# A four-layer graph network: adjacency and its transpose in one load, masks on GpSimd, and another order of work

## The chip, the cores and the metric

The kernel runs on one NeuronCore of a Trainium2 chip. The core has five engines with their own instruction streams: TensorE (PE in the profile; its weight loads are PEld), VectorE (DVE), ScalarE (ACT), GpSimd (POOL) and SyncE (SP), which here issues every transfer. They run their streams in order and wait for one another on semaphores. The metric is the time of one execution on the device, in microseconds; lower is better. Of several runs the median counts.

## The reference

128 graphs of 128 nodes with 512 features go through four graph attention layers. Each layer normalises its input, clips it at zero, makes a score for each pair of nodes, masks the scores by the adjacency, and adds the attention-weighted features to its input:

```python
h = jnp.maximum(_layernorm(x, axis=-1), 0.0)
x = x + _L0_gnn_ref(h, adj, W, a1, a2)          # 1 head, mask adj
h = jnp.maximum(_layernorm(x, axis=-1), 0.0)
x = x + _L1_gnn_ref(adj, h, W1, ..., W2, ...)   # 4 heads of 256, elu, then 1 head
h = jnp.maximum(_layernorm(x, axis=-1), 0.0)
x = x + _L2_gnn_ref(h, adj, w_src, w_dst, b)    # 1 head, mask adj + identity
h = jnp.maximum(_layernorm(x, axis=-1), 0.0)
x = x + _L3_gnn_ref(h, adj, W_proj, W_att, b)   # 8 heads of 64
```

Layer 1 has two attention layers (L1a with W1, L1b with W2), takes the softmax over the source nodes with `mask = (adj > 0) | eye`, and so needs the mask turned. Layer 3 takes its softmax over the second node, with the mask as it is; the kernel works on its scores turned as well.

## The kernel before

One graph fills the 128 partitions. The kernel is a software pipeline over graphs: each engine has a loop over `step`, and in it a fixed list of calls, each for the graph that stands so many steps behind. The whole schedule is that list, one for each engine, and the semaphores; nothing decides at run time.

```python
for step in range(G + SKEW):          # G = 128, SKEW = 12
    t = Turn(G, step)
    project_L1b_first_high(t, t.graph(5))   # graph number step - 5
```

I write `name(5)` for a call on the graph 5 steps behind. In a step `L0` works on graph 2 behind, `L1a` on 3 and 4, `L1b` on 5, `L2` on 6 and 7, `L3` on 9 to 11; the result of graph 12 behind is stored. PE stops being fully fed at the two ends of the loop, when the first graphs have not reached the late layers or the last ones have left the early layers.

Masks. GpSimd's `make_mask` (L1475) turns the int32 adjacency into 0 or -5e9 in bf16. `make_mask_loop` (L1482) clears the diagonal. PE turns both by a product with an identity: `turn_mask` (L450) and `turn_mask_L3` (L735), both into `bank_a`, which the products of L0 and L2 use too; ScalarE copies them to SBUF in `copy_mask` (L844) and `copy_mask_L3` (L990). The turned mask with cleared diagonal goes into `masked_L1a` and `masked_L1b`, the turned one into `masked_L3`.

Scores. For each attention the row of target scores of a graph goes from VectorE (`rows_...`, a 32x32 transpose) to DRAM (`send_...`) and comes back spread over all partitions (`spread_...`, L296 and L344): 64 KB for one head, 256 KB for L1a, 512 KB for L3. L3 needs a second round: VectorE takes eight masked maxima (`most_L3`, L1329), and their row goes out and back as `send_shift_L3`, `spread_shift_L3` (1 MB, L344). GpSimd adds the mask (`masked_...`), ScalarE does leaky relu and exp (`leaky_...`, `exp_...`), GpSimd subtracts the shift in L3 (`shift_L3`, L1540).

PE turns the exponentials (`turn_exp_L2` L493, `turn_prob_L1a` L579) and multiplies (`product_...`; L3's is L741, L1a's is L585). The wide projections (L432) split each float32 operand in a high and a low part: `hT_hi` on ScalarE, `hT_lo` on VectorE, three products for each weight. `scale_and_bias` (L1449, L1451, L1454) makes the layer norm's factors on GpSimd from VectorE's `stats` and `moments`.

At the end of L3, `result_L3` (L1372) on VectorE frees `bank_e`, for which `project_L3_last_high(9)` waits by its semaphore `out_read`; `out_L3` (L1558) adds the residual on GpSimd.

Of the kernel before, what the change touches and what calls it, by code (L numbers as in the profile page):

```python
# [14 lines left out]
SKEW = 12  # L15
# [39 lines left out]
def build(nc, x, adj, a0_w, a0_a1, a0_a2, w1, b1, w2, b2, attn_src, attn_dst, attn_b, w_proj, b_att, ident_in,  # L55
# [20 lines left out]
    with ExitStack() as ctx:  # L76
# [15 lines left out]
        identb = sb("identb", [P, P], BF16)  # L92
# [17 lines left out]
        PR, VR = 2, 2  # L110
        x_in = sb("x_in", [P, XR, D])
        adj_in = sb("adj_in", [P, XR, P], I32)
        mask = sb("mask", [P, MR, P], BF16)
        mask_loop = sb("mask_loop", [P, LR, P], BF16)
        mask_turned = sb("mask_turned", [P, TR, P], BF16)
        mask_flat_turned = sb("mask_flat_turned", [P, PR, P], BF16)
# [107 lines left out]
        def _(sp):  # L224
# [17 lines left out]
            def load_graph(s, i):  # L242
                sp.dma_start(x_in[:, s, :], x[i]).then_inc(sem(f"x_loaded{s}"), 16)
                sp.dma_start(adj_in[:, s, :], adj[i]).then_inc(sem(f"x_loaded{s}"), 16)
# [53 lines left out]
            def send_L0(g):  # L298
                send_one("L0", g, 0)
# [55 lines left out]
            for step in range(G + SKEW):  # L355
                t = Turn(G, step)
                load(t.graph(0))
                store(t.graph(12))
                spread_L2(t.graph(7))
                send_L0(t.later_graph(2))  # L360
                spread_L0(t.later_graph(2))
                send_L1b(t.graph(5))
                send_shift_L3(t.graph(10))
                spread_L1b(t.graph(5))
                spread_shift_L3(t.graph(10))
                send_L1a(t.graph(3))
                spread_L1a(t.graph(3))
                send_L3(t.graph(9))
                send_L2(t.graph(6))
                spread_L3(t.graph(9))  # L370
# [4 lines left out]
        def _(pe):  # L375
# [44 lines left out]
            pe.wait_ge(sem("setup_pe"), 2)  # L420
# [17 lines left out]
            def turn_mask(t, g):  # L438
                if g.live:
                    pe.wait_ge(sem("masks_made"), g.made())  # L440
                    if t.full:
                        pe.wait_ge(sem("x1_made"), g.made())
                    else:
                        pe.wait_ge(sem("mask_copied"), g.made(1))
                        pe.wait_ge(sem("L0_pT"), g.made())
                        pe.wait_ge(sem("x1_made"), g.made())
                        pe.wait_ge(sem("L2_pT"), g.made(5))
                        pe.wait_ge(sem("x3_made"), g.made(5))
                        pe.wait_ge(sem("flat_copied"), g.made(8))
                    mm(bank_a[:, 0:P], mask_loop[:, g.slot(LR), :], identb[:], start=True, stop=True)\  # L450
                        .then_inc(sem("mask_turned"), 1)

# [1173 lines left out]
```

## Time and profile before

| what | value |
|---|---|
| median of 3 runs | 3081.05 us (3080.08 to 3081.91) |
| the profiled execution's own time | 3083.84 us |
| its span, first to last instruction | 3082.1 us |
| PE busy | 2976.9 us, 97% of the span |
| PEld busy | 2746.1 us, 89% |
| VectorE busy | 2480.0 us, 80% |
| ScalarE busy | 2319.9 us, 75% |
| GpSimd busy | 2263.2 us, 73% |
| mean granted clock of TensorE | 0.977 of full speed |
| transfers | 355.71 MB, 115 GB/s on average |

The busy time of PE counts overlapping matmuls by their modelled ends, so the time that one costs is better read from the distance between the starts of two. The span is 1.7 us shorter than the execution's own time, and that is 2.8 us above the median; a sum made against the profiled execution has to be moved by the second figure.

### The profile page before, as it was taken

To read this page: it belongs to the slowest core of one execution; us is meant where nothing else is said; L and a number is where in the kernel's file an instruction comes from. 1 tells how busy PE (TensorE), PEld (TensorE's weight loads), DVE (VectorE), ACT (ScalarE), POOL (GpSimd) and SP (SyncE) were. 2 spreads that over 40 slices of the span, in tenths; PEclk is the share of its full clock that TensorE was granted. 3 is DMA by queue.
4 is the path that set the end of the run, shared out by engine and by line. 5 is a ranking of instruction groups with operands and counts; after the bars stand their busy time and mean duration, and the time that the engine had idled before them with its cause. 6 is when DMAs were issued, how large, how long until landed. Compare 5 with 4: busy or idle time off the path is not lost. (4 is left out here: it accounts for less than half of the span.)

```text
span 3082.1 us, 79166 instructions
## 1 busy us (share of the span) xinstructions
PE 2976.9 (97%) x21040; PEld 2746.1 (89%) x21040; DVE 2480.0 (80%) x8101; ACT 2319.9 (75%) x6433; POOL 2263.2 (73%) x3214
## 2 busy tenths in 40 slices
PE   7899999999999999999999999999999999999974
PEld 5789999999999999999999999999999999999964
DVE  3578888888888888888888888888888888888852
ACT  2567787778877788777787778877788777787752
POOL 3467777777777777777777777777777777777753
PEclk6999999999999999999999999999999999999985
DMA  5123333333333333333333333333333333333332
GB/s 195 34 69 123 117 119 122 108 124 118 119 123 106 125 117 119 122 109 122 118 119 121 108 122 120 120 118 112 121 120 119 118 110 122 120 120 119 96 107 93
DMA packets 205558, 355.71 MB, mean 115 GB/s; under 512 B 51904, under 2 KB 117568, under 8 KB 188736
## 3 DMA queue, kind: packets, MB, share of 16 engines
q1 hardware_dynamic: 205120, 350.66, 34.8%
q8 instruction: 179, 2.93, 0.4%
q14 instruction: 259, 2.12, 0.2%
HBM read 314.93 MB, written 35.59 MB: 114 GB/s over the span
## 5 line engine op out<-in xcount | busy, mean ns | idle before, releaser
L1454 POOL TENSOR_SCALAR rs<-mv,rs 128x1 f32<-128x1 f32 x512 | 357.6, 698 | 109.2 <-POOL rs L1451 108.8
L997 ACT ACTIVATE eT<-eT,tc 128x128 f32<-128x128 f32 x1024 | 314.1, 389 | 161.3 <-POOL eT L1534 161.3
L432 PE MATMUL bank_b<-w_hi,hT_hi 128*128 128x344 f32 x1536 | 419.8, 328 | 5.6 <-DVE g L1277 3.8
L432 PE MATMUL bank_c<-w_hi,g_hi 128*128 128x258 f32 x2048 | 414.1, 283 | 4.7 <-DVE x L1204 4.7
L432 PE MATMUL bank_c<-w_lo,g_hi 128*128 128x258 f32 x2048 | 414.5, 284 | 0.0
L432 PE MATMUL bank_b<-w_lo,hT_hi 128*128 128x344 f32 x1536 | 408.2, 320 | 0.0
L1329 DVE CUSTOM_DVE_ANT_0 t_all_L<-t_all_L,mask 128x128 f32<-128x128 f32 x1024 | 368.6, 413 | 27.0 <-DMA t_all_L<-t_dram_L 26.5
L432 PE MATMUL bank_b<-w_hi,hT_lo 128*128 128x344 f32 x1536 | 357.0, 327 | 0.0
L432 PE MATMUL bank_c<-w_hi,g_lo 128*128 128x258 f32 x2048 | 351.8, 284 | 0.0
L432 PE MATMUL bank_e<-w_hi,hT_hi 128*128 128x264 f32 x1024 | 341.1, 347 | 5.5 <-DVE out_sb L1372 5.4
L1540 POOL TENSOR_TENSOR eT<-eT,shift_all 128x512 f32<-128x512 f32 x256 | 331.1, 1294 | 4.6 <-ACT eT L997 4.4
L432 PEld LDWEIGHTS bank_c<-w_hi,g_hi 128*128 128x128 f32 x2048 | 318.4, 190 | 9.0 <-issue 9.0
L1451 POOL TENSOR_TENSOR rs<-rs,nhalf 128x1 f32<-128x1 f32 x512 | 293.5, 573 | 42.6
L432 PEld LDWEIGHTS bank_c<-w_lo,g_hi 128*128 128x128 f32 x2048 | 318.0, 190 | 0.0
L817 ACT ACTIVATE h<-x,rs 128x512 f32<-128x512 f32 x384 | 308.9, 805 | 6.4 <-PE bank_a L507 4.7
L741 PE MATMUL bank_e<-xa,eT 128*128 128x96 f32 x2048 | 286.0, 285 | 19.1 <-ACT eT L1004 19.0
L1534 POOL TENSOR_TENSOR eT<-shift_all,mask_flat_turned 128x512 f32<-128x512 f32 x256 | 294.3, 1172 | 8.4 <-DMA shift_all<-shift_dram 8.4
L1558 POOL TENSOR_TENSOR out_sb<-out_sb,x 128x512 f32<-128x512 f32 x128 | 165.7, 1294 | 181.8 <-DMA t_all_L1b<-t_dram_L1b 92.2
L432 PEld LDWEIGHTS bank_c<-w_hi,g_lo 128*128 128x128 f32 x2048 | 292.7, 190 | 0.0
L741 PEld LDWEIGHTS bank_e<-xa,eT 128*128 128x128 f32 x2048 | 258.2, 198 | 29.2 <-ACT eT L1004 21.4
L432 PE MATMUL bank_e<-w_hi,hT_lo 128*128 128x264 f32 x1024 | 280.8, 336 | 0.0
L432 PE MATMUL bank_e<-w_lo,hT_hi 128*128 128x264 f32 x1024 | 280.0, 287 | 0.0
(158 smaller groups left out, 8577.5 us busy)
## 6 DMA issues: line engine op xcount, KB each, us to landing
shift_all<-shift_dram SPq DMA_DIRECT2D x128, 1024.0 KB, 5.3
t_all_L<-t_dram_L SPq DMA_DIRECT2D x128, 512.0 KB, 3.7
x_in<-in_x SPq DMA_DIRECT2D x128, 256.0 KB, 2.6
t_all_L1a<-t_dram_L1a SPq DMA_DIRECT2D x128, 256.0 KB, 3.2
out<-out_sb SPq DMA_DIRECT2D x128, 256.0 KB, 3.1
t_all_L<-t_dram_L SPq DMA_DIRECT2D x256, 64.0 KB, 3.1
adj_in<-in_adj SPq DMA_DIRECT2D x128, 64.0 KB, 3.0
t_dram_L1a<-t_rows_L1a SPq DMA_DIRECT2D x512, 0.5 KB
```

The lines of the kernel that those rows point to most:

```text
L432: last = mm(bank[:, 0:width], a[:, c * P:(c + 1) * P], w[:, c, b * width:(b + 1) * width], start=(first and c == chunks[0] and n == 0), st ...
L741: last = mm(bank_e[:, i, k * KA:k * KA + NMIN], eT[:, head, :], xa[:, g.slot(VR), head * KA:head * KA + NMIN], start=True, stop=True)
L817: activation(h[layer][:], src, ACT.Relu, bias=rs[layer][:, 2:3], scale=rs[layer][:, 1:2])\
L997: last = activation(eT[:, k, :], eT[:, k, :], ACT.Prelu, bias=tc3[:, k:k + 1], alpha=SLOPE)
L1329: last = nc.vector.tensor_tensor_reduce(t_all["L3"][:, k, :], t_all["L3"][:, k, :], mask[:, g.slot(MR), :], 1.0, -3.0e38, ALU.add, ALU.max ...
L1451: tt(r, v, nhalf[:], ALU.pow).then_inc(sem(f"rs_made{layer}"), 1)
L1454: ts(b, mv[layer][:, 0:1], r, -1.0, ALU.mult, ALU.mult).then_inc(sem(f"rs_made{layer}"), 1)
L1534: tt(eT[:, half, :], shift_all[:, half, :], m, ALU.add).then_inc(sem(f"L3_masked{i}"), 1)
L1540: tt(eT[:, half, :], eT[:, half, :], shift_all[:, H3 + i * HB:H3 + (i + 1) * HB, :], ALU.subtract)\
L1558: tt(out_sb[:, g.slot(OR), :], out_sb[:, g.slot(OR), :], x3[:, g.slot(X3R), :], ALU.add)\
```

## The change

The host puts the adjacency and its transpose side by side (`in_adj`, 128x2x128 for a graph), so one load brings both, 128 KB for 64. `make_mask` masks both halves in one instruction of 256 elements. A new `turn_mask` on GpSimd clears the diagonal of the turned half. PE's two turns, ScalarE's two copies, the identity in bf16 and every wait on them are gone. `make_mask` now stands at graph 2 behind, `make_mask_loop` at 5.

The lists of calls are written in another order on all five engines, and SKEW is 11. Some calls belong to the step before now: on PE `project_L1b_first_high(4)` ends a step where `(5)` began one; on ScalarE and GpSimd `leaky_L1a`, `masked_L1a`, `leaky_L3_first`, `shift_L3_first`, `shift_L3_last` and `exp_L3_last` do the same.

```diff
-SKEW = 12
+SKEW = 11
-        adj_in = sb("adj_in", [P, XR, P], I32)
-        mask = sb("mask", [P, MR, P], BF16)
+        adj_in = sb("adj_in", [P, XR, 2, P], I32)
+        mask = sb("mask", [P, MR, 2, P], BF16)
...
-                    mm(bank_a[:, 0:P], mask_loop[:, g.slot(LR), :], identb[:], start=True, stop=True)\
-                        .then_inc(sem("mask_turned"), 1)
...
-                    mm(bank_a[:, 0:P], mask[:, g.slot(MR), :], identb[:], start=True, stop=True)\
-                        .then_inc(sem("flat_turned"), 1)
...
-                    activation(mask_turned[:, g.slot(TR), :], bank_a[:, 0:P], ACT.Copy).then_inc(sem("mask_copied"), 1)
...
-                    activation(mask_flat_turned[:, g.slot(PR), :], bank_a[:, 0:P], ACT.Copy).then_inc(sem("flat_copied"), 1)
...
-                    ts(mask[:, g.slot(MR), :], adj_in[:, s, :], BIG, -BIG, ALU.mult, ALU.add).then_inc(sem("mask_made"), 1)
+                    ts(mask[:, g.slot(MR), :, :], adj_in[:, s, :, :], BIG, -BIG, ALU.mult, ALU.add).then_inc(sem("mask_made"), 1)
...
+            def turn_mask(g):
+                if g.live:
+                    pool.wait_ge(sem("mask_made"), g.made())
+                    pool.wait_ge(sem("L1a_masked"), g.made(TR))
+                    pool.wait_ge(sem("L1b_masked"), g.made(TR))
+                    tt(mask_turned[:, g.slot(TR), :], mask[:, g.slot(MR), 1, :], offdiag[:], ALU.mult)\
+                        .then_inc(sem("turned_made"), 1)
...
+                targets_L3(t.graph(10))
                 moments_1(t.graph(3))
-                stats_2(t.graph(6))
+                sources_L3(t.graph(10))
...
+    ins["in_adj"] = np.ascontiguousarray(np.stack([adj, adj.transpose(0, 2, 1)], axis=2))
```

PE, from the last products of `project_L1b_last` to the products of L1a. `bank_c` belongs to L1b, `bank_e` to L3, `bank_b` to L1a. Before:

```order
L432 MATMUL bank_c<-w_hi,g_lo 128x258 x2
L450 MATMUL bank_a<-identb,mask_loop 128x128
L425 MATMUL bank_e<-ident,h 128x128 x4
L579 MATMUL bank_b<-ident,eB 128x128 x4
L741 MATMUL bank_e<-xa,eT 128x96 x4
L425 MATMUL bank_b<-ident,h 128x128 x4
L735 MATMUL bank_a<-identb,mask 128x128
L585 MATMUL bank_b<-pTB,xl 128x128 x8
L741 MATMUL bank_e<-xa,eT 128x96 x4
```

After (L701 is the product of L3, L554 the turn of L1a's probabilities, L560 its product):

```order
L430 MATMUL bank_c<-w_hi,g_lo 128x258 x2
L701 MATMUL bank_e<-xa,eT 128x96 x4
L554 MATMUL bank_b<-ident,eB 128x128 x4
L701 MATMUL bank_e<-xa,eT 128x96 x4
L423 MATMUL bank_b<-ident,h 128x128 x4
L560 MATMUL bank_b<-pTB,xl 128x128 x8
```

The two mask turns are gone, both products of L3 stand ahead of L1a's, and the turn of `h3` has moved ahead of `project_L1b_last`.

GpSimd, from `out_L3` to the end of the attention work of a step. Before:

```order
L1558 TENSOR_TENSOR out_sb<-out_sb,x 128x512
L1488 TENSOR_TENSOR e_L1b<-t_all_L1b,mask_turned 128x128
L1524 TENSOR_TENSOR g_lo<-g,g_hi 128x512
L1449 TENSOR_SCALAR rs<-mv 128x1
L1451 TENSOR_TENSOR rs<-rs,nhalf 128x1
L1454 TENSOR_SCALAR rs<-mv,rs 128x1
L1475 TENSOR_SCALAR mask<-adj_in 128x128
L1534 TENSOR_TENSOR eT<-shift_all,mask_flat_turned 128x512 x2
L1511 TENSOR_TENSOR eB<-t_all_L1a,mask_turned 128x512
L1540 TENSOR_TENSOR eT<-eT,shift_all 128x512
```

After; the calls `scale_2(6)`, `scale_3(8)` and `scale_0(1)` stand directly ahead of the first row:

```order
L1506 TENSOR_TENSOR out_sb<-out_sb,x 128x512
L1472 TENSOR_TENSOR g_lo<-g,g_hi 128x512
L1430 TENSOR_TENSOR mask_turned<-mask,offdiag 128x128
L1436 TENSOR_TENSOR e_L1b<-t_all_L1b,mask_turned 128x128
L1482 TENSOR_TENSOR eT<-shift_all,mask 128x512
L1436 TENSOR_TENSOR e_L<-t_all_L,mask 128x128
L1482 TENSOR_TENSOR eT<-shift_all,mask 128x512
L1488 TENSOR_TENSOR eT<-eT,shift_all 128x512
L1459 TENSOR_TENSOR eB<-t_all_L1a,mask_turned 128x512
L1488 TENSOR_TENSOR eT<-eT,shift_all 128x512
```

`e_L1b` and `e_L0` (the single row `e_L`) now stand behind three factors of the layer norm, `out_L3`, `g_lo` and the new row L1430, and both halves of the shift follow in the same step.

SyncE, the transfers of a step from the sending of L0's row on. Before:

```order
L274 DMA t_dram_L<-t_rows_L 4x32
L296 DMA t_all_L<-t_dram_L 128x128
L274 DMA t_dram_L1b<-t_rows_L1b 4x32
L333 DMA shift_dram<-shift_rows 16x32 x4
L296 DMA t_all_L1b<-t_dram_L1b 128x128
L344 DMA shift_all<-shift_dram 128x2048
```

After:

```order
L331 DMA shift_dram<-shift_rows 16x32 x4
L272 DMA t_dram_L1b<-t_rows_L1b 4x32
L272 DMA t_dram_L<-t_rows_L 4x32
L342 DMA shift_all<-shift_dram 128x2048
L294 DMA t_all_L1b<-t_dram_L1b 128x128
L294 DMA t_all_L<-t_dram_L 128x128
```

The 64 KB spreads of L1b and L0 stood ahead of the 1 MB spread; now both stand directly behind it, and it stands behind the sending of L0's row.

## Rows read from the trace of the kernel before

**Rows 1.** Busy us in stretches: PE, PEld, DVE, ACT, POOL; PE clock, DMA share.

```profile
1000.00:1400.00 400.00, 399.56 (x2872) 370.28 (x2872) 338.53 (x1103) 318.04 (x888) 310.28 (x440) 1.00 0.37 120
...
2950.00:3020.00 70.00, 43.61 (x238) 36.27 (x237) 33.89 (x132) 31.75 (x84) 36.42 (x45) 0.80 0.30 101
3020.00:3082.00 62.00, 26.97 (x123) 25.29 (x123) 13.22 (x78) 16.22 (x41) 19.42 (x17) 0.57 0.29 97
```

**Rows 2.** What PE itself waited for, 1000 to 2000 us, complete.

```profile
PE bank_e L425 <- ACT xa L982: 0.7, 2, 0.5
PE bank_e L741 <- ACT eT L1004: 0.7, 2, 0.4
```

**Rows 3.** PE in order of time, one step: start, duration, instruction.

```profile
1500.80 0.27 PE L493 MATMUL bank_a<-ident,p_L 128*128 128x128 f32 x1
...
1516.19 0.23 PE L450 MATMUL bank_a<-identb,mask_loop 128*128 128x128 bf16 x1
1516.29 0.63 PE L425 MATMUL bank_e<-ident,h 128*128 128x128 f32 x4
...
1518.60 0.22 PE L735 MATMUL bank_a<-identb,mask 128*128 128x128 bf16 x1
1518.65 2.00 PE L585 MATMUL bank_b<-pTB,xl 128*128 128x128 f32 x16
...
1523.41 0.27 PE L493 MATMUL bank_a<-ident,p_L 128*128 128x128 f32 x1
```

**Rows 4.** SyncE in order of time: the shift spreads of steps 131 and 137.

```profile
2951.19 0.34 SPq L344 DMA_DIRECT2D shift_all<-shift_dram  x1
...
3063.95 0.34 SPq L344 DMA_DIRECT2D shift_all<-shift_dram  x1
```

**Rows 5.** All engines in order of time, the last steps.

```profile
3030.82 0.56 PE L432 MATMUL bank_e<-w_hi,hT_hi 128*128 128x264 f32 x1 [1.18 <-DVE out_sb L1372]
...
3040.18 0.29 DVE L1329 CUSTOM_DVE_ANT_0 t_all_L<-t_all_L,mask 128x128 f32<-128x128 f32 x1 [4.14 <-DMA t_all_L<-t_dram_L]
...
3048.28 0.56 PE L432 MATMUL bank_e<-w_hi,hT_hi 128*128 128x264 f32 x1 [1.18 <-DVE out_sb L1372]
...
3077.42 0.76 DVE L1372 SCALAR_TENSOR_TENSOR out_sb<-bank_e,rcE 128x256 f32<-128x256 f32 x2
```

**Rows 6.** GpSimd in groups by line, 1000 to 2000 us: busy us, mean ns.

```profile
L1534 POOL TENSOR_TENSOR eT<-shift_all,mask_flat_turned 128x512 f32<-128x512 f32 x88 | 100.4, 1163 | 0.0
L1558 POOL TENSOR_TENSOR out_sb<-out_sb,x 128x512 f32<-128x512 f32 x45 | 58.3, 1296 | 51.0 <-DMA t_all_L1b<-t_dram_L1b 34.8 <-DVE out_sb L1372 16.1
L1524 POOL TENSOR_TENSOR g_lo<-g,g_hi 128x512 fp32r<-128x512 f32 x44 | 56.8, 1291 | 39.6 <-ACT g_hi L950 39.6
...
L1482 POOL TENSOR_TENSOR mask_loop<-mask,offdiag 128x128 bf16<-128x128 bf16 x44 | 18.7, 425 | 0.0
L1475 POOL TENSOR_SCALAR mask<-adj_in 128x128 bf16<-128x128 int32 x44 | 13.2, 300 | 3.5
```

**Rows 7.** GpSimd in order of time, within one step.

```profile
1515.52 1.04 POOL L1517 TENSOR_TENSOR eB<-eB,sumB 128x512 f32<-128x512 f32 x1 [1.04 <-DVE sumB L1271]
...
1519.89 0.23 POOL L1449 TENSOR_SCALAR rs<-mv 128x1 f32<-128x1 f32 x1
...
1521.21 0.43 POOL L1488 TENSOR_TENSOR e_L<-t_all_L,mask 128x128 f32<-128x128 f32 x1
```

**Rows 8.** VectorE's stretch begins, in the order of time of all engines.

```profile
1507.48 1.23 DVE L1259 TENSOR_TENSOR xl<-bank_b,b_row 128x1032 f32<-128x1032 f32 x1 [0.54 <-issue]
```

**Rows 9.** VectorE in order of time, the end of that stretch.

```profile
1515.54 1.16 DVE L1329 CUSTOM_DVE_ANT_0 t_all_L<-t_all_L,mask 128x128 f32<-128x128 f32 x1
...
1517.42 0.65 DVE L1097 BATCH_NORM_STATS2 bn<-x_in 128x6 f32<-128x512 f32 x1
```

**Rows 10.** Transfers by kind, whole span: count, KB each, median us to landing.

```profile
shift_all<-shift_dram SPq DMA_DIRECT2D x128, 1024.0 KB, 5.3
...
t_all_L1b<-t_dram_L1b SPq DMA_DIRECT2D x128, 64.0 KB, 3.1
```

## What I predict, before seeing the result

> **What bounds the kernel now.** I read the busy time by stretches first. In the steady part PE is busy for 399.56 of 400 us, at the full granted clock; only the end is different, where it is busy for 43.6 of 70 and 27.0 of 62 us [rows 1]. A modelled busy time can hide waits, so I looked next at what PE itself waited for: 1.4 us in 1000 us, four waits in all [rows 2]. Then at the order of time on PE: the same instruction comes again after 1523.41 - 1500.80 = 22.61 us, with no gap in between [rows 3]. So the kernel is two problems. For about 118 steps PE sets the time, one step costs what its instructions cost, and no other engine is waited for. At the end the step is set by something else: the 1 MB spreads of steps 131 and 137 are 3063.95 - 2951.19 = 112.8 us apart, 18.8 us a step [rows 4], while PE is idle for half of it.
>
> **Term 1, PE's own work.** Two turns of a mask go. What each costs is the distance from its start to the next: 1516.29 - 1516.19 = 0.10 us and 1518.65 - 1518.60 = 0.05 us, 0.15 us a step [rows 3]. The upper bound is what they are busy for, 0.23 + 0.22 = 0.45 us, but matmuls overlap, as those same distances show, and I do not take it; the lower bound is 0.10, if the rounded second distance hides nothing. Nothing is added on PE; the rest is moved. 118 x 0.15 = 17.7 us less (12 to 24 for 0.10 to 0.20), and the step comes to 22.46 us.
>
> **Term 2, the end of the loop.** In the last steps one circle sets the pace: `project_L3_last_high` starts at 3030.82 and again at 3048.28, 17.46 us [rows 5]. It goes: projection, `rows_L3`, send, 512 KB spread, `most_L3` on VectorE (its first maximum at 3040.18 [rows 5]), and behind the first half of the maxima, because the list has it there, `targets_L3`; then `values_L3`, the turn of `h3`, both products, `result_L3`, projection. In the new list `targets_L3(10)` and `sources_L3(10)` stand ahead of the maxima, and the values no longer wait for a spread. What is late next is the long chain of a graph through L3: from the projection at 3048.28 through both rounds to the end of `result_L3` at 3077.42 + 0.76 = 3078.18, 29.9 us [rows 5]. In the new lists shift, exp and product close this circle in two steps, so a step is at least 15.0 us. Six steps at 15.0 for 18.8 would be 23 us; the first two of them still carry L1b and L2, so I count four: 4 x 3.8 = 15 us less (0 to 23). Fewer steps (SKEW) give nothing by themselves: a graph passes the same instructions. For the beginning of the loop I take no change: the chains of L1a and L1b that set it keep their order, and VectorE and GpSimd have the new work under PE's. I allow 5 us either way.
>
> **What is added elsewhere.** GpSimd gets one mask of 128x128 bf16, 0.43 us by the same operation in `make_mask_loop`, and `make_mask` doubles from 0.30 us to at most 0.60 [rows 6]. It is busy for 310 of 400 us [rows 1], so 0.7 us in a step of 22.5 fits. ScalarE loses two copies and VectorE nothing; neither sets the step. The load grows by 64 KB in a transfer share of 0.37 [rows 1], and stands two steps ahead of its use. These I cost at nothing, as long as PE is what everything waits for; the cover is examined next.
>
> **Does the new order keep PE fed?** This is the step that can fail. In the new lists there is a circle that goes through VectorE, GpSimd and ScalarE once a step without PE; if it is longer than 22.46 us, it is the step. I add it up in three legs.
> Leg 1, VectorE from `values_L1a` to `moments_2`. The old stretch from `values_L1a` (1507.48 [rows 8]) to the end of the maxima (1517.42 [rows 9]) is 9.94 us and holds nearly the same calls. The new one adds a statistics pass (0.65 as the one at 1517.42 [rows 9]), a subtraction of 512 columns that I estimate like it, and small instructions (0.7 by my estimate): 12.0 us. But in the old stretch one maximum took 1.16 us [rows 9] where others take 0.29 [rows 5], and it started 0.02 us after GpSimd's product of the probabilities L1517, which took 1.04 [rows 7]. In the new order that product needs a reciprocal which stands behind the maxima on VectorE, so it cannot fall on them. Without this and its echo in the next one, 10.7 us.
> Leg 2, GpSimd from `scale_2` to `masked_L0`: three `scale_and_bias` of 1521.21 - 1519.89 = 1.32 us [rows 7], then 1.30, 1.29, 0.43, 0.43, 1.16 and 0.43 us [rows 6, 7], 9.0 us.
> Leg 3, from there to `values_L1a` again: leaky 0.4 and maximum 0.3 for L0, then `columns_L2`, two passes of about 0.7, and 0.2 of small ones, all by my estimate from passes of 512 columns at 0.65 [rows 9]: 2.3 us, or 2.8 if the passes meet `masked_L3_first`, which runs at that moment.
> Sum: 10.7 + 9.0 + 2.3 = 22.0 us to 12.0 + 9.0 + 2.8 = 23.8 us, against 22.46. I take the low end, 22.0 to 22.5, because the one long conflict is ordered away; then PE waits for nothing, or a tenth.
> The conflict is first this row: the maximum with two inputs in SBUF waited out the GpSimd instruction. The Trainium skill, SBUF - State Buffer, section "Who interferes with whom", states it as a rule: a VectorE instruction with two SBUF inputs and a GpSimd instruction that reads SBUF exclude each other, and the second is blocked for the whole of the first. It speaks against the change, which gives GpSimd one more such instruction a step; by it the price is at most that instruction's 0.43 us where it falls on such a pass, and the sum would stay between the ends above.
>
> **A transfer in front.** The 1 MB spread lands 5.3 us after its issue, the 64 KB of L1b 3.1 us [rows 10]. In the new order the small one is issued right behind the large one, whose issue takes 0.34 us [rows 4]. If it lands on its own, it has 2 us to spare before GpSimd comes to `masked_L1b`; that is leg 2 up to there, 3.96 + 1.30 + 1.29 + 0.43 = 7.0 us after `moments_2`, less some 1.1 us (my estimate) from the end of the row to the issue, so 5.9 us. If it lands behind the large one, that is 4.9 to 5.8 us after its issue (the large one's 5.3, and a spread of up to 6.2 that I allow), just in time.
> The Trainium skill, DMA: Bandwidth & Descriptors, section "Queues, rings and completion order", says that on each DMA engine the descriptors of one queue are consumed in ring order. By that rule the second case holds, at a margin of 0.1 to 1 us; in the kernel before the small one stood ahead, so its rows do not test it.
>
> **The sum.** 3083.84 of the profiled execution, less 17.7, less 15, is 3051; the median of the runs stands 2.8 us lower: 3048 us.
>
> **Rivals.**
> (a) PE stays fed and both terms come, 3034 to 3062 us: half. For it speak that VectorE and GpSimd are idle for 15 and 22% of the steady part [rows 1], against it that the circle above is as long as the step.
> (b) Only one of the two terms comes, because the end is held by something else, or PE waits 0.1 to 0.2 us a step: 3062 to 3074 us, 14%.
> (c) What PE loses in work it gets back in waits, 0.2 to 0.3 us a step: 3075 to 3087 us, 8%. This also is where "the work does not matter" would show.
> (d) Slower: the circle through VectorE and GpSimd is longer than PE's step. It decides from a wait of 32.7 / 118 = 0.28 us a step on, that is from a circle of 22.74 us. At the middle of the bounds, 22.9, PE waits 0.5 us a step: 3048 + 59 = 3107 us; at the upper end 23.8, 1.3 us a step: some 3200. It would show as PE waiting before `turn_exp_L1b` or `product_L0`, whose inputs ScalarE makes behind `masked_L0` and `leaky_L3_last`. 24%.
> (e) The transfers are not kept apart but queued: the small spread lands behind the large one, and later than I allow. Each 0.1 us beyond the margin is 12 us; it would be part of (b), (c) or (d), and I have it in their chances.
> (f) Both terms at their upper ends and the beginning shorter too, below 3034: 4%.
>
> **How the numbers follow.** A difference of 0.2%, 6.2 us, is about what a measurement of this kernel can tell. (a), (b) and (f) are faster: 0.68. (c) is the same: 0.08. (d) is slower: 0.24. The time is that of (a). The range goes from 3030, where 3 in 100 of (f) are left out, to 3110, where half of (d) is; it holds about 85 in 100. For (a) alone it is 3034 to 3062.
>
> **What would show it.** Right: the distance between equal instructions on PE is 22.4 to 22.5 us, and its waits in 1000 us stay below 5 us; the 1 MB spreads of the last steps are 15 to 16 us apart; GpSimd's busy time a step is 0.5 to 0.7 us more, ScalarE's 0.5 less; no maximum of `most_L3` takes over 0.6 us. Wrong: PE waits once in each step at the same instruction. If that is for ScalarE's `pT` copies, (d) holds; if GpSimd's `e_L1b` waits for its transfer, (e). If the last steps are still 17 to 19 us apart, term 2 fails, and what VectorE waits for there names the circle that I did not see.

## The result, and the profile after

The changed kernel takes 3140.61 us (median of 4 runs, 3140.41 to 3142.38) for 3081.42: a ratio of 1.019, 95% interval 1.0177 to 1.0203. It is slower, by what I had as rival (d). The profiled span is 3138.9 us.

By the loads of the adjacency (the 16th and the 128th of each trace) the budget is: up to the 16th 1.8 us more; a step from there to the 128th 23.28 us for 22.675, 68 us more in 112 steps; from the 128th to the end 13 us less. The sum is 57 us, the difference of the spans. So the end became shorter, as forecast (9.4 of the 13 us lie in its last six steps, see below), and the steady part went the other way.

Busy time by stretches of the kernel after, columns as in [rows 1]:

```profile
1000.00:1400.00 400.00, 392.14 (x2757) 353.12 (x2755) 340.27 (x1077) 304.99 (x821) 286.59 (x448) 1.00 0.36 117
```

What PE itself waited for, 1000 to 2000 us of the kernel after, complete:

```profile
PE bank_a L458 <- ACT pT_L L812: 12.5, 43, 0.3
PE bank_c L626 <- ACT p_L1b L806: 3.3, 10, 0.4
```

And what its weight loads waited for in the same stretch:

```profile
PEld bank_a L458 <- ACT pT_L L812: 46.8, 43, 1.1
...
PEld bank_c L626 <- ACT p_L1b L806: 17.6, 43, 0.7
```

PE was busy for 399.56 of 400 us in [rows 1] and is for 392.14. Its list shows 15.8 us of waits in 43 steps, 0.4 us a step; the weight loads, which run ahead of the matmuls, show 64. PE waits once a step, for the copies `pT` and the exponentials that ScalarE makes: the sign that the prediction gave for (d). Four instructions of PE in order of time, kernel after: the turns of the exponentials of L1b and L0, then their products:

```profile
1516.07 0.33 PE L626 MATMUL bank_c<-ident,p_L1b 128*128 128x128 f32 x1
...
1517.52 0.33 PE L446 MATMUL bank_a<-ident,p_L 128*128 128x128 f32 x1
1517.68 1.12 PE L638 MATMUL bank_c<-xl,pT_L1b 128*128 128x512 f32 x2
...
1519.10 1.10 PE L458 MATMUL bank_a<-h,pT_L 128*128 128x512 f32 x2 [0.29 <-ACT pT_L L812]
```

The two products in the kernel before:

```profile
1507.22 1.02 PE L663 MATMUL bank_c<-xl,pT_L1b 128*128 128x512 f32 x2
1508.08 1.02 PE L479 MATMUL bank_a<-h,pT_L 128*128 128x512 f32 x2
```

From L638 to L458 it is 1.42 us, where it was 0.86. Against the kernel before, the distances between the starts are longer by 0.27 us ahead of L626, 0.14 from there to L638, 0.56 from L638 to L458 and 0.08 behind it (means of 1000 to 2000 us). That is about 1.0 of 23.24 us, and PE's own work would be 22.2 us.

Now the circle that the prediction added up. VectorE in the kernel after, one turn of it:

```profile
1495.45 1.23 DVE L1201 TENSOR_TENSOR xl<-bank_b,b_row 128x1032 f32<-128x1032 f32 x1
...
1501.76 0.29 DVE L1271 CUSTOM_DVE_ANT_0 t_all_L<-t_all_L,mask 128x128 f32<-128x128 f32 x1
...
1502.52 1.01 DVE L1289 SCALAR_TENSOR_TENSOR shift_cols<-most 128x8 f32<-128x8 f32 x1
...
1512.84 1.16 DVE L1233 TENSOR_TENSOR g_lo<-g,g_hi 128x512 fp32r<-128x512 f32 x1
...
1516.85 1.00 DVE L1087 CUSTOM_DVE_ANT_0 product<-h,s_row,attn_b_all 128x512 bf16<-128x512 f32 x1
...
1518.69 1.23 DVE L1201 TENSOR_TENSOR xl<-bank_b,b_row 128x1032 f32<-128x1032 f32 x1
```

and GpSimd, in the same stretch:

```profile
1502.46 1.04 POOL L1465 TENSOR_TENSOR eB<-eB,sumB 128x512 f32<-128x512 f32 x1 [1.00 <-DVE sumB L1213]
...
1506.76 0.22 POOL L1391 TENSOR_SCALAR rs<-mv 128x1 f32<-128x1 f32 x1 [2.37 <-DVE mv L1046]
...
1512.17 1.28 POOL L1472 TENSOR_TENSOR g_lo<-g,g_hi 128x512 fp32r<-128x512 f32 x1
1513.41 0.88 POOL L1430 TENSOR_TENSOR mask_turned<-mask,offdiag 128x128 bf16<-128x128 bf16 x1
...
1515.76 0.42 POOL L1436 TENSOR_TENSOR e_L<-t_all_L,mask 128x128 f32<-128x128 f32 x1
1516.14 1.16 POOL L1482 TENSOR_TENSOR eT<-shift_all,mask 128x512 f32<-128x512 f32 x1
```

From `values_L1a` to itself is 1518.69 - 1495.45 = 23.24 us, the step. GpSimd waits 2.37 us for `moments_2`; from there on it waits for no other engine up to `masked_L0`, and its end is waited for by ScalarE and VectorE. It is the circle, closed. Inside it, three blocks (an instruction stands still while one on the other of the two engines runs): the subtraction of 8 columns L1289 takes 1.01 us where it takes 0.17 undisturbed, and ends with GpSimd's product of the probabilities L1465; GpSimd's turn of the mask takes 0.88 us where 0.43 is usual, behind a `g_lo` of 1.16 us on VectorE which itself was blocked; `columns_L2` takes 1.00 us, for 0.73 in the kernel before, and loses 0.27. The eight maxima are undisturbed, 0.28 to 0.29 us each. That much I had right.

At the end of the loop, SyncE's 1 MB spreads of steps 131 and 137, kernel after (answering to [rows 4]):

```profile
3017.14 0.38 SPq L342 DMA_DIRECT2D shift_all<-shift_dram  x1
...
3120.47 0.34 SPq L342 DMA_DIRECT2D shift_all<-shift_dram  x1
```

They are 103.3 us apart for 112.8; the last four steps take 15.8 to 16.1 us each. That is 9.4 us less. The other 3.6 of the 13 lie between the 128th load and step 131 (98.4 us for 102.2).

One execution of kernel e14 below took 14384 us, with PE's instructions several times as long from beginning to end; its other four took 3165 to 3169 us, and its rows are read from a second run of the same kernel, e15.

### The profile page after: what moved, and what is told of

It reads as the page before. It is cut to its first block and busy times, and to the rows that moved or that the text cites. A ratio compares the mean times of both kernels' runs of the same rounds, so it can differ in the third digit from the quotient of the medians.

```text
span 3138.9 us, 77888 instructions
## 1 busy us (share of the span) xinstructions
PE 3003.4 (96%) x20784; PEld 2700.4 (86%) x20784; DVE 2548.4 (81%) x8100; ACT 2301.1 (73%) x6177; POOL 2148.1 (68%) x3342
## 5 line engine op out<-in xcount | busy, mean ns | idle before, releaser
L430 PE MATMUL bank_b<-w_hi,hT_hi 128*128 128x344 f32 x1536 | 469.2, 360 | 5.4 <-DVE g L1219 3.6
L430 PE MATMUL bank_c<-w_hi,g_hi 128*128 128x258 f32 x2048 | 425.5, 289 | 2.3 <-DVE x L1146 2.3
L1391 POOL TENSOR_SCALAR rs<-mv 128x1 f32<-128x1 f32 x512 | 115.1, 225 | 386.5 <-DVE mv L1046 365.5
L942 ACT ACTIVATE eT<-eT,tc 128x128 f32<-128x128 f32 x1024 | 323.5, 390 | 31.4 <-POOL eT L1482 31.4
L430 PEld LDWEIGHTS bank_b<-w_hi,hT_hi 128*128 128x128 f32 x1536 | 278.1, 189 | 66.8 <-issue 66.2
L1482 POOL TENSOR_TENSOR eT<-shift_all,mask 128x512 f32<-128x512 f32 x256 | 298.2, 1166 | 12.3 <-DMA shift_all<-shift_dram 12.3
L701 PE MATMUL bank_e<-xa,eT 128*128 128x96 f32 x2048 | 273.0, 278 | 20.3 <-ACT eT L949 12.1
L701 PEld LDWEIGHTS bank_e<-xa,eT 128*128 128x128 f32 x2048 | 258.8, 198 | 21.6 <-ACT eT L949 17.5
L430 PEld LDWEIGHTS bank_b<-w_lo,hT_hi 128*128 128x128 f32 x1536 | 274.6, 189 | 0.0
L1039 DVE BATCH_NORM_STATS2 bn<-x 128x6 f32<-128x512 f32 x384 | 263.9, 687 | 4.4
```

The costliest lines, as they stand in the source:

```text
L430: last = mm(bank[:, 0:width], a[:, c * P:(c + 1) * P], w[:, c, b * width:(b + 1) * width], start=(first and c == chunks[0] and n == 0), st ...
L701: last = mm(bank_e[:, i, k * KA:k * KA + NMIN], eT[:, head, :], xa[:, g.slot(VR), head * KA:head * KA + NMIN], start=True, stop=True)
L942: last = activation(eT[:, k, :], eT[:, k, :], ACT.Prelu, bias=tc3[:, k:k + 1], alpha=SLOPE)
L1039: nc.vector.bn_stats(bn[layer][:], src).then_inc(sem(f"bn_made{layer}"), 1)
L1391: ts(v, mv[layer][:, 1:2], EPS, None, ALU.add).then_inc(sem(f"rs_made{layer}"), 1)
L1482: tt(eT[:, half, :], shift_all[:, half, :], m, ALU.add).then_inc(sem(f"L3_masked{i}"), 1)
```

## Experiments

In the table, a step is the time between the 16th and the 128th load of the adjacency by 112, and "end" the time between the 1 MB spreads of the last step and the sixth before it. Ratios are against the kernel before, which ran beside each.

| kernel | us | ratio (95%) | step | end |
|---|---|---|---|---|
| before | 3081.42 | | 22.68 | 112.8 |
| after | 3140.61 | 1.019 (1.0177 to 1.0203) | 23.28 | 103.3 |
| e1 new masks, old order | 3117.12 | 1.0113 (1.0098 to 1.0129) | 22.95 | 113.9 |
| e2 old masks, new order | 3096.97 | 1.0049 (1.0032 to 1.0065) | 22.93 | 101.5 |
| e3 after, reciprocal later | 3087.02 | 1.0016 (1.0007 to 1.0025) | 22.84 | 102.9 |
| e4 after, turn early | 3097.54 | 1.0049 (1.0034 to 1.0064) | 22.94 | 100.0 |
| e5 after, both moves | 3046.21 | 0.9887 (0.9873 to 0.99) | 22.50 | 102.4 |
| e6 e5, product_L0 later | 3074.97 | 0.9978 (0.9969 to 0.9987) | 22.72 | 101.2 |
| e7 e1, masks in idle time | 3050.53 | 0.9901 (0.9888 to 0.9915) | 22.38 | 114.3 |
| e8 after, small spreads first | 3322.1 | 1.0789 (1.0773 to 1.0806) | 24.74 | 102.2 |
| e9 before, targets early | 3068.83 | 0.9953 (0.9941 to 0.9966) | 22.59 | 110.7 |
| e10 e7, targets early | 3044.15 | 0.9873 (0.986 to 0.9887) | 22.39 | 113.2 |
| e11 e5, copy first | 3070.65 | 0.996 (0.9946 to 0.9974) | 22.72 | 101.5 |
| e12 e10, shift ahead of L2 | 3107.6 | 1.0081 (1.0067 to 1.0095) | 22.92 | 109.2 |
| e13 e12, exp ahead too | 3108.74 | 1.0087 (1.007 to 1.0104) | 22.94 | 109.0 |
| e14, e15 e5, shift behind L2 | 3165.89 | 1.0281 (1.0263 to 1.0298) | 23.46 | 107.4 |

**e1, the new masks alone.** The old lists, SKEW 12, without the mask turns of PE and ScalarE, and on GpSimd:

```diff
                 make_mask_loop(t.graph(3))
+                turn_mask(t.graph(3))
                 prob_L1a(t.graph(4))
```

> The new masks in the old order of work (SKEW 12, turn_mask(3) on GpSimd right behind make_mask_loop(3)). Theory T (the new order makes a circle through VectorE, GpSimd and ScalarE of 23.23 us, longer than PE's own step; the masks as such save PE 0.15 us a step): the old order is PE-bound at 22.61 us, so this one is at 22.46 us a step, 17.7 us less than before, about 3064 us, and PE's waits stay at a few us in 1000. Rival M (the loss comes from the masks: GpSimd's extra mask, or the doubled load): it is slower than before, up to the whole loss, about 3140 us. Rival W (the PE work taken away was hidden by other matmuls and is worth nothing): 3081 us, no change.

Measured: 3117 us, slower, as only rival M had it. PE waits once a step, 12.0 us in 44 times, for a copy of ScalarE (`xa`, from `values_L3`). All engines of e1 in order of time, the place:

```profile
1506.26 0.42 POOL L1422 TENSOR_TENSOR mask_loop<-mask,offdiag 128x128 bf16<-128x128 bf16 x1
...
1506.65 0.48 POOL L1430 TENSOR_TENSOR mask_turned<-mask,offdiag 128x128 bf16<-128x128 bf16 x1
1506.77 0.51 DVE L1271 CUSTOM_DVE_ANT_0 t_all_L<-t_all_L,mask 128x128 f32<-128x128 f32 x1
...
1507.63 0.15 DVE L1257 COPY tc<-bank_e 128x8 f32<-128x8 f32 x1
...
1507.98 0.60 ACT L934 ACTIVATE xa<-bank_e 128x512 f32<-128x512 f32 x1 [1.37 <-DVE tc L1257]
...
1508.73 0.63 PE L423 MATMUL bank_e<-ident,h 128*128 128x128 f32 x4 [0.26 <-ACT xa L934]
```

And in the kernel before:

```profile
1515.19 0.16 DVE L1315 COPY tc<-bank_e 128x8 f32<-128x8 f32 x1
...
1515.55 0.60 ACT L982 ACTIVATE xa<-bank_e 128x512 f32<-128x512 f32 x1 [1.14 <-DVE tc L1315]
```

The copy `tc` starts 8.03 us after `values_L1a` (1499.60); in the kernel before it was 7.71 (1515.19 and [rows 8]). The 0.32 us are 0.09 that `most_L1a` started later, behind the wider mask (0.40 for 0.30 us), and 0.22 of the maximum that took 0.51 for 0.29 beside the turn of the mask. The normal step is 22.92 for 22.61, the same 0.31. So the kernel before had a second chain as long as PE's: VectorE to `tc`, `xa`, `turn_h3`. There `xa` was ready at 1516.15 (1515.55 + 0.60) and PE started the turn at 1516.29 [rows 3], 0.14 us later. This is no margin: in e1, where the profile shows PE waiting for that copy, the turn starts 0.15 us after it (1508.58 to 1508.73). The 0.14 us is what the hand-over takes in every step of both kernels from 1000 to 2000 us, and PE's list of waits [rows 2] does not show it. So the kernel before was already held there. I had read "PE waits for nothing" as room.

**e2, the new order alone.** The new lists with the old masks: PE's turns behind `project_L1b_last` and `turn_h1`, the copies on ScalarE, `make_mask_loop(3)` first on GpSimd.

> The old masks (PE turns both, ScalarE copies both) in the new order of work, SKEW 11. Theory T: nearly all of the loss comes with the order, so 3115 to 3150 us; GpSimd's turn of the mask (0.88 us of the circle) is gone, which alone would give back up to 0.7 us a step if nothing else were near, but ScalarE's two copies and PE's two turns come back. A step of 22.7 to 23.3 us, with waits of PE in it. Rival M (the masks make the loss): about 3070 us, 22.6 us a step and the shorter end.

Measured: 3097 us, below the 3115 to 3150 us that I gave for theory T, with 22.93 us a step as it had it. The order alone costs 16 us; the masks in this order cost another 44 (3140.61 for 3096.97), as they cost 36 in the old one. Both halves of the change lengthen a step, each for reasons of place. `shift_cols` is blocked in e2 too, 1.02 us, and so is GpSimd's instruction right behind its `g_lo`, here `masked_L1b` (0.88 for 0.43 us): these blocks belong to the order. The circle's middle leg, from `scale_2` to `masked_L0`, is 9.07 us in e2 and 9.43 in the changed kernel, so the added mask costs 0.36 us there; the common step is 22.88 and 23.24 us, 0.36 apart as well.

**e3, e4 and e5: two calls moved in the changed kernel.** On VectorE (e3) and on GpSimd (e4); e5 has both.

```diff
-                recip_L1a(t.graph(4))
                 most_leaky_L3(t.graph(10))
                 rows_shift_L3(t.graph(10))
+                recip_L1a(t.graph(4))
```
```diff
                 make_mask(t.later_graph(2))
+                turn_mask(t.graph(3))
                 scale_2(t.graph(6))
...
                 g_lo_last(t.graph(4))
-                turn_mask(t.graph(3))
```

> The changed kernel with one call moved on VectorE: the reciprocal of L1a behind the row of L3's shift, so that GpSimd's product of the probabilities can no longer fall on the subtraction that makes this row (1.01 us for 0.17). Theory T: this 0.84 us is on the circle; the step falls from 23.23 by up to 0.84, to 22.4 to 22.7 us, 3050 to 3085 us; less if the block only moves to the next VectorE pass or if GpSimd, starting its product later, comes late to its scale factors. Rival Q (PE waits for transfers or for ScalarE, whatever VectorE does): 3140 us, no change.

> The changed kernel with one call moved on GpSimd: the turn of the mask (0.88 us there) ahead of the factors of the layer norms, where GpSimd waits 2.4 us for VectorE's moments. Theory T: it is on the leg from the moments to masked_L0; the step falls by 0.4 to 0.9 us, to 22.46 to 22.8 us, 3050 to 3090 us. Rival Q: no change, 3140 us.

> The changed kernel with both moves at once: the reciprocal of L1a behind the row of L3's shift on VectorE, the turn of the mask ahead of the layer-norm factors on GpSimd. Alone they left a step of 22.80 and 22.88 us for 23.23. Theory T: the circle is then shorter than PE's own step. What PE's instructions cost in the new order is 23.23 less about 1.0 us of stalls, 22.2 us; so a step of 22.2 to 22.5 us, 3020 to 3055 us, faster than before. Rival P (a second limit, not through VectorE: product_L0 waits for the copy of its weights on ScalarE, because turn_exp_L0 now stands behind the low projection and leaky_L3_last ahead of the copy; a stall of 0.5 us a step that no move on VectorE or GpSimd takes away): 22.7 to 22.8 us a step, 3075 to 3090 us.

Measured: 22.84, 22.94 and 22.50 us a step, that is 0.44, 0.34 and 0.78 less; e3 and e4 gained less than their theories had it, e5 what it had. The two add up, as they must on one circle. Its three legs (medians of 1000 to 2000 us: `values_L1a` to `scale_2`, `scale_2` to the end of `masked_L0`, from there to `values_L1a`):

| kernel | leg 1 | leg 2 | leg 3 | sum |
|---|---|---|---|---|
| after | 11.30 | 9.43 | 2.51 | 23.24 |
| e3 | 10.82 | 9.47 | 2.51 | 22.79 |
| e4 | 11.31 | 9.07 | 2.51 | 22.88 |
| e5 | 10.83 | 9.11 | 2.51 | 22.45 |

e3 shortens leg 1 and e4 leg 2, each alone. In e4 the mask takes 0.43 us at its new place, but the block did not leave the leg with it. It falls on `masked_L1b`, as GpSimd of e4 shows:

```profile
1516.95 1.28 POOL L1472 TENSOR_TENSOR g_lo<-g,g_hi 128x512 fp32r<-128x512 f32 x1
1518.19 0.89 POOL L1436 TENSOR_TENSOR e_L1b<-t_all_L1b,mask_turned 128x128 f32<-128x128 f32 x1
```

In e3 `shift_cols` is back at its own time, and part of the gain is given back at once, because the product of the probabilities now stands beside `columns_L0`. VectorE of e3 in order of time:

```profile
1501.73 0.17 DVE L1289 SCALAR_TENSOR_TENSOR shift_cols<-most 128x8 f32<-128x8 f32 x1
...
1503.35 0.91 DVE L1087 CUSTOM_DVE_ANT_0 product<-h,s_row 128x512 bf16<-128x512 f32 x1
...
1504.19 0.87 DVE L1087 CUSTOM_DVE_ANT_0 product<-h,t_row 128x512 bf16<-128x512 f32 x1
```

Those two took 0.67 and 0.69 us in the changed kernel: 0.84 - 0.24 - 0.18 = 0.42, where 0.44 was measured. e5 is 1.1% faster than before. PE's own list there, 1000 to 2000 us, is one line:

```profile
PE bank_a L458 <- ACT pT_L L812: 1.2, 5, 0.3
```

Yet PE is held once a step here too. `product_L0` starts 0.14 us after the end of the copy `pT_L` (1519.10 + 0.26 to 1519.50), as it does in the changed kernel, where the list shows the wait. In the kernel before these two were 0.87 us apart:

```profile
1519.10 0.26 ACT L812 ACTIVATE pT_L<-bank_a 128x128 f32<-128x128 f32 x1
...
1519.50 1.10 PE L458 MATMUL bank_a<-h,pT_L 128*128 128x512 f32 x2
```

So in e5 the circle still sets the step, as far as its rows show.

**e6 and e11: the stall at `product_L0`.** In e5 it is 1.00 us from L638 to L458 for 0.86. e6 takes the product behind `project_L3_first`, e11 the copy ahead of the leaky relu on ScalarE:

```diff
-                product_L0(t, t.later_graph(2))
                 project_L3_first(t, t.graph(9))
+                product_L0(t, t.later_graph(2))
```
```diff
+                pT_L0(t.later_graph(2))
                 leaky_L3_last(t.graph(10))
-                pT_L0(t.later_graph(2))
```

> As the one with both moves, and on PE product_L0 behind project_L3_first (1.86 us later). Theory T: product_L0 waits for nothing in the one with both moves already, so this brings nothing, and at worst makes the residual of L0 on VectorE late: 3020 to 3070 us. Rival P: the stall of 0.5 us at product_L0 is what is left, and it goes: 22.2 to 22.4 us a step, 3020 to 3045 us, 30 to 60 us less than the one with both moves.

> The changed kernel with both moves (3046 us, 22.46 us a step), and on ScalarE the copy of L0's turned weights ahead of leaky_L3_last. What is left of the stall at product_L0 is 0.2 us a step by the trace. Theory P2: the stall goes, 22.25 us a step, 3020 to 3030 us. Rival C: ScalarE waits 0.7 to 0.9 us for PE's turn before it can go on to leaky_L3_last, the shift of L3 and masked_L1a on GpSimd come later by as much and with them the maxima of L1a on VectorE, whose margin is 0.2 to 1.0 us: 3046 to 3100 us.

Measured: 29 and 24 us more than e5; e6 outside both of its ranges, e11 in that of rival C. The stall goes in both, and another comes: in e6 VectorE waits for `product_L0` (7.4 us in 44 steps, 0.17 each), in e11 for the leaky relu of L1a (7.8 us, 0.18 each), both on the circle. That these waits make up the loss was not tested. Rival P's stall was real in the changed kernel, but it was what the circle left over, not a second limit.

**e7, the new masks where GpSimd waits.** From e1:

```diff
-                make_mask_loop(t.graph(3))
-                turn_mask(t.graph(3))
...
+                make_mask(t.later_graph(1))
                 out_L3(t.graph(11))
                 masked_L1b(t.graph(5))
+                make_mask_loop(t.graph(3))
+                turn_mask(t.graph(3))
                 g_lo_last(t.graph(4))
                 scale_0(t.later_graph(1))
-                make_mask(t.later_graph(1))
```

> The new masks in the old order, as the first experiment (3117 us, 22.92 us a step), but the three mask instructions stand where GpSimd waits anyway: make_mask ahead of out_L3 (idle 1.14 us there), the two of 128 columns ahead of g_lo_last (idle 0.94 us). Theory B (in the old order PE's turn_h3 had no margin against a chain of VectorE, GpSimd and ScalarE from values_L1a to columns_L3 and xa; the first experiment made it 0.32 us longer, 0.10 by the wider mask and 0.2 by a maximum that the turn of the mask blocked): both are gone and the wider mask is off the chain altogether, so at least 0.3 us a step less: 22.4 to 22.6 us, 3055 to 3080 us. Rival M (GpSimd has too much work or the doubled load hurts): 3110 to 3120 us.

Measured: 3050.5 us, better than theory B had it, and 67 us less than e1 by the place of three instructions. Most steps take 22.29 us. GpSimd is busy for 323.77 of 400 us, 310.28 before [rows 1] and 286.59 in the changed kernel, and PE is busy for all 400: the work on GpSimd was never too much, and neither was the doubled load. Rival M falls. `xa` is now ready 0.37 us ahead of the turn of `h3`.

**e8, the small spreads ahead of the large one.**

```diff
-                spread_shift_L3(t.graph(10))
                 spread_L1b(t.graph(5))
                 spread_L0(t.later_graph(2))
+                spread_shift_L3(t.graph(10))
```

> The changed kernel with the 1 MB spread behind the two of 64 KB on SyncE. Theory T: GpSimd did not wait for the small transfers, so 3140 us, no change within 0.3%. Rival E (the small spreads land late behind the large one and hold the step): 10 to 60 us less.

Both were wrong: 180 us more. Transfers of e8 by kind (count, KB, median us to landing):

```profile
shift_all<-shift_dram SPq DMA_DIRECT2D x128, 1024.0 KB, 7.0
...
t_all_L1b<-t_dram_L1b SPq DMA_DIRECT2D x128, 64.0 KB, 3.0
```

One of GpSimd's waits in e8, 1000 to 2000 us:

```profile
POOL eT L1482 <- DMA shift_all<-shift_dram: 52.6, 38, 2.1
```

These are 38 waits of 1.4 us on average, and the step is 1.46 us longer. In the changed kernel the two land 4.7 and 4.5 us after their issue, in [rows 10] 5.3 and 3.1. Whichever stands second lands later. In the changed kernel GpSimd had no idle time ahead of the instructions that read them, L1482 and L1436, so nobody waited for either. That the large one stands first is what its lists need.

**e9 and e10: `targets_L3` and `sources_L3` ahead of the maxima**, in the kernel before and in e7.

```diff
+                targets_L3(t.graph(10))
+                sources_L3(t.graph(10))
                 most_L1a(t.graph(4))
...
-                sources_L3(t.graph(10))
                 most_L3_first(t.graph(10))
-                targets_L3(t.graph(10))
```

> The kernel before with one change: targets_L3 and sources_L3 on VectorE stand ahead of the maxima, so the values of L3 no longer wait for the 512 KB spread. It tests the mechanism of term 2 (the end of the loop) alone. Theory T2: the last steps get shorter, at most by the 15 us that I gave to the whole new order (which ended 13 us shorter); 3066 to 3075 us. In the steady part the copy of the values and turn_h3 come 0.3 us earlier, where PE had no wait to lose: nothing. Rival: the end is held by the way of L3's shift through its 1 MB spread, which this edit does not shorten: 3080 to 3083 us.

> The new masks in the old order with the mask instructions in GpSimd's idle time (3050.5 us), and targets_L3 and sources_L3 ahead of the maxima. Theory T2: another 5 to 15 us less, 3035 to 3046 us, the fastest kernel so far. Rival: 3050 us, as above.

Measured (e9): 15 us less than the kernel before beside it, as expected in size, and for the larger part not where expected. The six last steps are 110.7 us, 2.1 less (113.2 in e10 for 114.3 in e7). The mechanism of term 2 is there in the last two of them alone, which L2 has left: 32.0 us for 35.0, and 31.9 for 35.1 in e10. The two steps ahead of these stay near 20 us each, where the new order has 15.8. Most of the gain, 0.09 us a step x 112 = 10 us, is in the steady part: `tc` comes 4.35 us after `values_L1a` for 7.71, `xa` is ready 1.37 us ahead of the turn of `h3`, and the common step is 22.54 us for 22.61. By this difference PE was held for 0.07 us a step in the kernel before, and its list did not show it. e10 has the same lists and the new masks: 22.39 for 22.59, so the masks that PE no longer turns are worth 0.20 us a step (0.27 between undisturbed steps, 22.54 and 22.27). It is the fastest kernel by its median; the intervals of e5 and e10 overlap.

**e12 to e15: what paces the end.** The chain of waits of e9, in the last steps, in order of time:

```profile
2985.86 0.74 DVE product L1145
...
2987.50 0.87 DMA t_dram_L<-t_rows_L
2988.37 4.62 issue
...
2993.03 0.41 POOL e_L L1488
...
2995.01 1.23 POOL eT L1540
...
2996.27 0.64 ACT eT L1004
...
2996.95 2.04 PE bank_e L741 x8
...
3000.16 2.10 PE bank_e L432 x8
3002.25 1.49 PE bank_a L507 x2
```

`columns_L2`, its way through DRAM, `masked_L2`, then `shift_L3_first` behind it on GpSimd, exp, product, and the projection and `product_L2` of the next step. The chain of the kernel before has the same pieces. e12 moves the shift ahead of `masked_L2` in e10, e13 also the exp ahead of `leaky_L2`; e14 puts the shift back behind `masked_L2` in e5.

```diff
+                shift_L3_first(t.graph(11))
                 masked_L2(t.graph(7))
                 scale_3(t.graph(8))
-                shift_L3_first(t.graph(11))
```

> As the last but one (new masks in GpSimd's idle time, targets early, old order otherwise; 3044 us), and on GpSimd shift_L3_first ahead of masked_L2. Moving the targets of L3 had changed nothing at the end of the loop: the six last steps took 110.7 us (113.3 here) as 112.8 before, 102.4 to 103.3 with the new order. Theory S: the end is paced by a circle that I had not named: projection and product_L2 on PE, columns_L2 on VectorE, the transfer of L2's scores, masked_L2, scale_3 and then shift_L3_first on GpSimd, exp, product_L3_first, result_L3 and the projection again. With the shift ahead of masked_L2 it is cut: the six last steps take 102 to 106 us, some 8 to 11 us less in all, 3032 to 3040 us if the steady part stays at 22.3 us. Rival: the end is held by something else of the new order (SKEW 11, or both halves in one step); the six steps stay at 110 to 113 us. In the steady part the move delays masked_L2 and scale_3 by 1.3 us, which may cost up to some 0.2 us a step; the six last steps tell the theories apart either way.

> As the last one (3107.6 us; six last steps 109.2 us), and on ScalarE exp_L3_first ahead of leaky_L2, as in the new order. In the last one the chain at the end still went from masked_L2 to leaky_L2 on ScalarE and from there to exp_L3_first behind it. Theory S (the circle runs through L2's transfer by whatever stands behind it in a list): now it is cut on both engines, and the six last steps take 102 to 105 us, as with the new order. Rival: they stay at 109 us or more, and something else of the new order shortens the end. The steady part is disturbed as in the last one, so the whole time says little: 3090 to 3105 us.

> The reverse test, on the changed kernel with both moves (3046 us, six last steps 102.4 us): shift_L3_first leaves its place at the end of GpSimd's list and stands behind masked_L2 of the next step, as in the old order. Theory S (the end is paced by what waits behind L2's transfer on GpSimd): the six last steps go back to 108 to 113 us. Rival R (another part of the new order shortens the end; cutting the circle in the old order gave only 4 us of the 10): they stay at 102 to 105 us. The steady part is likely to be longer by some tenths a step, since the exponentials of L3's first half now come a step later for PE: 3050 to 3120 us in all.

> The kernel of the run before once more (3165.9 us in its undisturbed executions; the profiled one took 14384 us, with TensorE slowed all along, and its rows say nothing), for the sake of its rows. The same two theories: six last steps of 108 to 113 us (S) or of 102 to 105 us (R).

Measured: the end went from 113.2 to 109.2 and 109.0 us, and from 102.4 to 107.4 the other way, e12 and e15 fell between the two ranges given, e13 where its rival had it. The steady part cost more each time than I had allowed (0.53 us a step in e12, for 0.2; 3166 us in all in e14, for at most 3120). The circle through L2's transfer is worth 4 to 5 of the 10 us, by both tests; what gives the rest is open. The steady part shows the blocks once more. VectorE and GpSimd of e12, in order of time:

```profile
1505.87 1.04 POOL L1465 TENSOR_TENSOR eB<-eB,sumB 128x512 f32<-128x512 f32 x1 [1.25 <-DMA t_all_L<-t_dram_L]
1505.89 1.17 DVE L1271 CUSTOM_DVE_ANT_0 t_all_L<-t_all_L,mask 128x128 f32<-128x128 f32 x1
...
1506.86 1.32 POOL L1488 TENSOR_TENSOR eT<-eT,shift_all 128x512 f32<-128x512 f32 x1
...
1506.98 1.35 DVE L1271 CUSTOM_DVE_ANT_0 t_all_L<-t_all_L,mask 128x128 f32<-128x128 f32 x1
```

One shift moved behind the product stretches another maximum from 0.29 to 1.35 us, and the step goes from 22.39 to 22.92 us.

## Why the prediction was wrong, step by step

**The step that failed** is the choice of an end: "I take the low end, 22.0 to 22.5, because the one long conflict is ordered away; then PE waits for nothing, or a tenth." The circle takes 23.24 us. The sum of the legs held its bounds of 22.0 to 23.8. Leg 1, 10.7 to 12.0, is 11.3 with its hand-over; leg 2, 9.0, is 9.4 (1516.18 - 1506.76); leg 3, 2.3 to 2.8, is 2.5. The conflict was not ordered away: the reciprocal that released GpSimd's product had moved behind the maxima, and with it the product fell on a later pass in the list, `shift_cols`. The block was 0.84 us, as long as on a maximum [rows 9], though the pass itself is 16 times smaller. e3 shows it: without it leg 1 is 10.8, and the step 0.44 us less. That alone would not have brought the low end, since e3 still has 22.8. The rest lies in leg 2: 0.45 us of a block behind GpSimd's `g_lo`, and 0.20 of the layer norm's factors, 1.42 and 1.44 us for two of the three where I had 1.32. Part of it is hidden by instructions that overlap.

**The price of the conflict.** For the added mask I had "at most that instruction's 0.43 us". What it costs by itself on the circle is 0.36 us (leg 2 with it and without it, e2 and e4), so that was right. The 0.88 us that it takes in the changed kernel hold the block of 0.45 that stands behind `g_lo` with or without it. At its old place in e1 it cost 0.22 us on a maximum. The Trainium skill's rule (SBUF — State Buffer, "Who interferes with whom"), that the second of two such instructions waits out the first, agrees with each of these rows; I cited it and then priced one collision instead of all that the new list has, with the added mask or without.

**Costed at nothing.** "These I cost at nothing, as long as PE is what everything waits for." e1 measures them: 0.31 us a step, and as PE's own saving of some 0.27 us was to be had too, the masks at the old places cost 0.6 us (22.92 us a step for 22.29 in e7). The cover was not there: the kernel before was already held at `turn_h3`, by the hand-over from `xa`. The reading "PE sets the time, one step costs what its instructions cost, and no other engine is waited for" was wrong by 0.07 us a step in size, and wholly as a margin.

**Term 1** was right in sign and small in size: 0.20 to 0.27 us a step instead of 0.15 (e9 and e10), inside the bound of 0.45. In the changed kernel none of it could show. In e7 and e10 it does.

**Term 2** came near in size (13 us less for 15 from the last load on, but 9.4 in the six steps that I had counted; steps of 15.9 us for "at least 15.0") and was in the main wrong in mechanism. The circle that I named, `targets_L3` behind the maxima, is worth 3 us, in the last two steps (e9, e10). I had read it there [rows 5] and carried it over to four. In the two steps ahead, the chain of waits of the kernel before names the circle through `masked_L2`, worth 4 to 5 us; the rest is open. That the sum came near was luck.

**A transfer in front.** The small spread landed behind the large one, 4.5 us after its issue for 3.1, and GpSimd did not wait for it, as the case "just in time" said; rival (e) did not happen.

**The likeliest number** came true in kernels that the change is not: 3046 us in e5 and 3044 us in e10, for 3048 predicted. They differ from the change, or from e1, by two and by five calls moved. In e5 the step of 22.46 us agrees with the forecast by luck: PE's saving was larger than I had it, and the circle took the difference.

## What to carry to other kernels

A kernel whose tensor engine waits for nothing in its list can have a second circle of the same length. Before adding work to another engine, look for the instruction on PE whose input was ready last. Compare the distance with the one that it has where PE is seen to wait: 0.14 us was no margin here, 0.37 and 0.87 were. When a call moves, ask what each instruction of the other engine now runs beside, one by one, and price all collisions, not the one that went away: here moving two calls was worth 94 us and moving three masks 67 us, with the work unchanged. Put added work on an engine right ahead of its long waits, not where it fits the list's logic.

## What the runs showed of the hardware

A VectorE pass over 128x8 elements with both inputs in SBUF waits for a running GpSimd instruction as long as a pass over 128x128 does: 0.17 us became 1.01. The block passes on to whatever GpSimd instruction stands next: behind `g_lo` the turn of the mask, 0.43 us alone, took 0.88, and with the turn moved away `masked_L1b`, 0.43 alone, took 0.89 at the same place. A PE instruction that is held by a ScalarE copy, `xa` or `pT_L`, starts 0.14 us after the copy's end (before, e1, the changed kernel, e5), also where the profile lists no wait. A 1 MB spread lands 4.7 us after its issue when it stands first (the changed kernel), 5.3 with one of 64 KB directly ahead (before [rows 10]), and 7.0 with two (e8), far more than their 128 KB would take by its own rate (0.6 us by 4.7 us for 1 MB, an estimate); why is open.
